# Rotated query and key parts: one copy in memory and twelve repeating strip reads per pair, in place of repeated copies and four reads

## The reference

```
x = x + attention(layernorm(x))
x = x + experts(layernorm(x))

# attention
q, k = rope(q), rope(k)
scores  = q @ k.T / sqrt(8), only where 0 <= i - j <= 63
weights = softmax(scores);  out = (weights @ v) @ Wout
```

## Time and profile before

| | us |
|---|---|
| median of 3 runs | 603.52 (600.43 to 605.98) |
| the profiled execution | 604.68 |
| its span, first to last instruction | 602.5 |

### The profile page before, as it was taken

One profiled execution on the slowest core, in us unless ns is written; L12 is line 12 of the kernel. 1 busy time (PEld: TensorE's weight loads), 2 busy tenths in 40 slices (PEclk: granted clock), 3 DMA queues, 4 the chain that ended last, 5 costly groups with the idle time before them and its releaser, 6 DMA issues.

```text
span 602.5 us, 20827 instructions
## 1 busy us (share of the span) xinstructions
PE 513.2 (85%) x7427; PEld 423.3 (70%) x7427; DVE 424.7 (70%) x1297; ACT 323.1 (54%) x832; POOL 343.0 (57%) x362
## 2 busy tenths in 40 slices
PE   3558997989988798887669889999989999999756
PEld 2336665766666566665545589999989999998544
DVE  5666799779999899966676366756666676664264
ACT  3336775767777677655546225455446555454200
POOL 8520113276666566655777507777777777777600
PEclk9659998989999999977899979999999999999977
DMA  7889998887877665520000134543534554541198
GB/s 254 234 234 249 250 248 235 225 268 212 240 231 208 210 209 151 137 66 25 21 12 10 36 99 140 150 123 108 164 119 140 171 155 149 170 118 49 24 394 292
DMA packets 79417, 98.33 MB, mean 163 GB/s; under 512 B 12097, under 2 KB 59999, under 8 KB 79216
## 3 DMA queue, kind: packets, MB, share of 16 engines
q1 hardware_dynamic: 65280, 82.92, 47.2%
q0 software_dynamic: 9216, 12.02, 6.4%
q10 hardware_dynamic: 4848, 2.40, 1.4%
HBM read 50.00 MB, written 54.30 MB: 173 GB/s over the span
## 4 chain that ended last, share of the span: by engine, by line
PE 38%; DVE 6%; DMA 5%; issue 4%; POOL 3%; ACT 2%; SPq 0%; POOLq 0%; DVEq 0%; ACTq 0%
PE banks L1115 18%; PE banks L1141 12%; DMA rload<-pair_results 3%; PE banks L1126 3%; POOL expert_slots L490 2%; DVE mx L1239 1%; PE banks L932 1%; DMA pair_results<-yout,yidx 1%; PE banks L1050 1%; POOL pair_results L618 1%; PE banks L1167 0%; DMA xg<-expert_slots 0%; SPq L440 0%; PE banks L874 0%; ACT yout L805 0%
## 5 line engine op out<-in xcount | busy, mean ns | idle before, releaser
L618 POOL DMA_INDIRECT pair_results<-yout,yidx x160 | 159.3, 996 | 67.0 <-issue 38.1
L490 POOL DMA_INDIRECT expert_slots<-xfe,sidx x128 | 127.8, 998 | 89.7 <-issue 38.9
L1115 PE MATMUL banks<-xgT_parts,wgu_parts 128*128 128x320 f32 x768 | 131.3, 320 | 1.9 <-DVE hact L1506 1.7
L1115 PEld LDWEIGHTS banks<-xgT_parts,wgu_parts 128*128 128x128 f32 x768 | 113.9, 190 | 4.6 <-DVE hact L1506 2.3
L1239 DVE TENSOR_REDUCE mx<-banks 128x8 f32<-128x1024 f32 x64 | 78.0, 1219 | 21.0 <-PE banks L882 21.0
L1506 DVE TENSOR_TENSOR hact<-hact,banks 128x320 f32<-128x320 f32 x128 | 56.6, 482 | 43.0 <-ACT hact L786 42.1
L805 ACT ACTIVATE yout<-banks,ypair 128x128 f32<-128x128 f32 x160 | 44.8, 372 | 76.2 <-PE banks L1141 73.8
L655 ACT ACTIVATE pt<-banks 128x512 f32<-128x512 f32 x128 | 69.3, 593 | 27.9 <-PE banks L913 26.6
L1141 PE MATMUL banks<-wdn,hact 128*128 128x128 f32 x640 | 76.6, 275 | 1.1 <-DVE hact L1506 1.1
L1141 PEld LDWEIGHTS banks<-wdn,hact 128*128 128x128 f32 x640 | 75.0, 192 | 1.3 <-issue 1.3
L786 ACT ACTIVATE hact<-banks 128x320 f32<-128x320 f32 x128 | 53.5, 452 | 33.1 <-PE banks L1115 31.4
(11 more groups left out here) (154 smaller groups left out, 945.5 us busy)
## 6 DMA issues: line engine op xcount, KB each, us to landing
expert_slots<-xg SPq DMA_DIRECT2D x32, 325.0 KB, 4.8
xg<-expert_slots SPq DMA_DIRECT2D x32, 325.0 KB
pair_results<-zero SPq DMA_DIRECT2D x32, 256.0 KB
rload<-pair_results SPq DMA_DIRECT2D x16, 512.0 KB, 8.9
kS<-rotated_keys SPq DMA_DIRECT2D x32, 240.0 KB
qS<-rotated_queries SPq DMA_DIRECT2D x32, 192.0 KB
wgu<-in_L_ffn_wg_dram SPq DMA_DIRECT2D x32, 128.0 KB
wgu<-in_L_ffn_wu_dram SPq DMA_DIRECT2D x32, 128.0 KB
```

Source lines behind the costliest of these rows:

```text
L490: g.indirect_dma_start(out=slots_d, out_offset=bass.IndirectOffsetOnAxis(ap=sidx[:, m % NB, j, k:k + 1], axis=0), in_=xfe[:, m % NB, j, k, ...
L618: g.indirect_dma_start(out=pairs_d, out_offset=bass.IndirectOffsetOnAxis(ap=yidx[:, c, j:j + 1], axis=0), in_=yout[:, c, j, :], in_offset= ...
L1115: last = mm(bank[2 + 2 * w + h][:, 0:CH], wgu_parts[:, e.b, wp, w, h * P:(h + 1) * P], xgT_parts[:, e.b, xp, ch * CH:(ch + 1) * CH], start ...
```

## The change

The tensors in memory hold three parts in place of six. `write_part` writes each part of queries and keys once. Each strip of 48 rows is read with three transfers, of 24, 16 and 8 rows, in place of one. For the queries (`Q_ROWS`), these repeat one part three times, the next twice, the last once: the source has an outermost dimension of stride zero. For the keys (`K_ROWS`), they read parts 0 to 2, then parts 0 and 1, then part 0. The six products are the same, in another order of rows. TensorE's wait counts twelve transfers per pair.

```diff
 NPART = 6
-Q_SLOTS = ((0, 1, 3), (3, 1, 2), (5, 1, 1))
-K_SLOTS = ((1, 2, 3), (0, 4, 2), (2, 1, 1))
+NSPLIT = 3
+Q_ROWS = ((0, 3, 0, False), (3, 2, 1, False), (5, 1, 2, False))
+K_ROWS = ((0, 3, 0, True), (3, 2, 0, True), (5, 1, 0, True))
 PEN_ROW = NPART * DH
+STRIP_LOADS = NS * (len(Q_ROWS) + len(K_ROWS))
...
-    q_d = nc.dram_tensor("rotated_queries", [NP, NPART, DH, NS, NG * PW], BF16, kind="Internal").ap()
-    k_d = nc.dram_tensor("rotated_keys", [NP, NPART, DH, NS, NG * (WIN + PW)], BF16, kind="Internal").ap()
+    q_d = nc.dram_tensor("rotated_queries", [NP, NSPLIT, DH, NS, NG * PW], BF16, kind="Internal").ap()
+    k_d = nc.dram_tensor("rotated_keys", [NP, NSPLIT, DH, NS, NG * (WIN + PW)], BF16, kind="Internal").ap()
...
             def write_part(m, a):
-                for w, (to, (first, step, count), lead) in enumerate(((q_d, Q_SLOTS[a], WIN), (k_d, K_SLOTS[a], 0))):
+                for w, (to, lead) in enumerate(((q_d, WIN), (k_d, 0))):
                     if w and a == 0:
                         sp.wait_ge(S.key_lead, m + 1)
-                    rows = to[m, first:first + step * (count - 1) + 1:step].rearrange("n d s (g t) -> (d s g) n t", g=NG)
-                    sp.dma_start(rows, parts[:, m % 2, a, w, lead:].unsqueeze(1)
-                                 .broadcast_to([P, count, WIN + PW - lead])).then_inc(S.qk_written, 16)
+                    sp.dma_start(to[m, a].rearrange("d s (g t) -> (d s g) t", g=NG), parts[:, m % 2, a, w, lead:])\
+                      .then_inc(S.qk_written, 16)
...
-                for strip, given in ((qS, q_d), (kS, k_d)):
+                for strip, given, rows in ((qS, q_d, Q_ROWS), (kS, k_d, K_ROWS)):
                     for s in range(NS):
-                        sp.dma_start(strip[STRIP * s:STRIP * s + PEN_ROW, m % NX].rearrange("p g t -> p (g t)"),
-                                     given[m, :, :, s].rearrange("r d t -> (r d) t")).then_inc(strips[m % NX], 16)
+                        for first, count, part, following in rows:
+                            at = STRIP * s + first * DH
+                            if following:
+                                source = given[m, part:part + count, :, s]
+                            else:
+                                source = given[m, part:part + 1, :, s].broadcast_to([count, DH, NG * PW])
+                            sp.dma_start(strip[at:at + count * DH, m % NX].rearrange("p g t -> p (g t)"), source)\
+                              .then_inc(strips[m % NX], 16)
...
-                        pe.wait_ge(strips[p % NX], 16 * 2 * NS * (p // NX + 1))
+                        pe.wait_ge(strips[p % NX], 16 * STRIP_LOADS * (p // NX + 1))
```

## The result

The changed kernel takes 627.74 us (median of 4 runs, 619.03 to 630.78), the kernel before 602.89 beside it (600.43 to 605.98): a ratio of 1.033, 95% interval 1.026 to 1.040. The ratio compares executions in the chip's faster state alone, for the changed kernel 625.40 and 619.03 of the four, with a mean of 622.2. By it the change costs 20 us. The forecast was 628, 23 us more than before; that 627.74 lies so close to it is luck in part. The profiled execution took 625.4 us, its span is 623.2 for 602.5, and these twenty-one microseconds can be followed from the prediction's own rows.

A forecast was written before the change was run, and what follows sets the result against it. Transfers were taken to bound the early stage, VectorE the later. Six early gaps +17, gap 6 to 7 +3, six later gaps +3, the end nothing: +23 on 604.7 gives 628 us, likeliest case's range 604 to 654.

The forecast's parts named there:

- What bounds the kernel: Attention pairs: transfers fill the DMA engines early (0.94 busy at 60 to 75 us), VectorE paces the later stage.
- The spread decides the sign: Strip reads: query reads run on three, two and eight engines, joined key reads on 12, 16 and 8; slower, total +23 us.
- The price of the narrow rows: Strip reads per pair: first engine's query rows 6.9 us, key rows 2.0; 9.0 us in place of 3.3.
- The early term: Six gaps between strip reads, pair 0 to 6: 17.4 us each, with weight loads 108.7 against 91.8, +17 us.
- The account: Gap between pairs' strip reads: one engine's reads, pieces and writes plus 1.9 us; 13.3 us before, 17.4 early after.
- The late gaps: Gap 6 to 7: 18.0 us against 14.9, +3; six gaps to pair 13: 16.7 against 16.2, +3.
- The end: After pair 13: 9.0 us of reads and 2 of latency fit 10.8 us of slack, so nothing; expert stage moves later unchanged.
- Issue: SP's queue: twelve strip reads for four at 0.42 us, last one 3.4 us later, hidden behind over 5 us of engine work.
- the rival without a difference: Reads spread evenly, but later issue costs 12 us over seven early steps against 11 saved: 605 us; chance 0.12.
- The faster rival: Reads spread over twelve or more engines, early gap 11.7 us, TensorE's strip stalls go: 597 us; chance 0.10.

The follow-up runs named there:

- the keys kept apart: Changed kernel with one unused row in memory behind each part of the keys, so part and dimension can't be joined into one count: 673.09 us, ratio 1.117.
- eight engines each: Changed kernel with the rows of each strip block reordered, head dimension (8) outermost, same writes, twelve reads and bytes: 629.43 us, ratio 1.044.
- half the writes: Kernel before, each part written once; four 48-row reads take the previous pair's rows instead of repeats, so output isn't the reference's: 596.74 us, ratio 0.989.
- the twelve even reads: Kernel before with its full writes, each 48-row strip read replaced by plain reads of 24, 16 and 8 rows: 613.67 us, ratio 1.018.
- the tiny reads: Kernel before with eight additional reads per pair, 16 rows of 64 B each to an unused tile, two ahead of each strip read: 631.49 us, ratio 1.042.

## Why the prediction was right, point by point

**What bounds the kernel.** Right: where the queue's pace changes, the first scores change with it, and the expert loop moves by 23.5 us, of which 2.8 come back by the end.

**The spread decides the sign.** Right, and shown from three sides: the packet counts fit to the last one (53536, 52800 with the keys kept apart, 53504 with eight engines each), a load on one engine that nobody waits for costs 1.034, and two badly divisible plain reads cost 1.035 with none of the change's other parts. That the narrow reads start from the same engine each time was assumed in the prediction. No record names an engine, but the numbers of packets under way show it: three while two reads are issued, then two.

**The price of the narrow rows.** The early term was +15.1 for +17, but that doesn't make the price right, since the terms overlap. With the keys narrow too, the five early gaps without weight loads average 20.2 us; less 8.4 for pieces, writes and latency that leaves 11.8 us for 313 kB, 38 us per MB, less than the undisturbed 40.5: part of the reading must go on during the other terms. By the packet records, the rows of that version take 13.6 us per pair (median, from the start of the first to the end of the last), 43 us per MB. In the changed kernel they take 9.1 to 11.2 us, waits for issues among them, with a median of 9.6 for the forecast 9.0. So the term was a little low. The account runs some 1.3 us short of the mean early gap where no engine is overloaded (14.6 for 13.3 before, 13.1 for 11.7 with half the writes) and is close where one is (16.9 for 17.4). The gap that it was held against, 13.2, is the shortest of the early ones, and it counts four fill pieces of 1.2 us per gap where SP issues five; whether that is what is short isn't shown. So it is luck in part that the total came out nearer than its terms.

**The late gaps.** +6.0 for +3: mis-sized. The sum let the strips land 2 us after 9.0 of reads and the last write 1.9 us after its issue. In the trace TensorE has the strips 11.8 to 13.4 us after the first issue: 1.5 us pass before the first row starts and some 0.6 after the last one. From the end of the last write's issue to the next strip read, 1.3 to 4.2 us pass, 3.2 on average for 2.5 before; 1.9 was the value of one quiet pair. That writes too stand behind narrow reads is the likely reason: behind pair 13's, from 245.1 to 247 us, the records show mostly one to three packets of the queue under way.

**The end.** The last three pairs gave 1.7 us back, which the sum didn't have (1.3 from the first read of pair 15 to its first scores, 0.4 in the two gaps before), and 2.2 of the 22.9 that are left at the last pair's first scores came back by the end.

**Issue.** Put at nothing because the first engine's load hides it: 3.4 us later for eight issues. It was 4.5 (5.8 for 1.3 in a quiet pair), since the query reads are issued at 0.59 us on average and not at 0.42. How much of the loss it would be alone was forecast as 1.7 us per early step in the rival without a difference; the twelve even reads show 1.9, with some uneven load among it. In the changed kernel the strips still land some 6 us after the last issue, so there the engine ends last. But the two are not shares of one sum: issues with little or no uneven load (1.018, and 1.042 with the tiny reads) and load alone (1.034, 1.035) each cost much, and with the load spread over eight engines the dearer issues took its place (1.044).

**The faster rival.** Its mechanism is real, and its size as worked out (596.7 for 597), where the reads stay as they are. What made it lose is the price of repeating on the reading side.

## What to carry to other kernels

Before splitting a transfer or repeating its source, look at the outermost count on both sides: three copies in front mean three engines, however many bytes there are, and a mean share over sixteen engines falls while the full one sets the pace. Where one queue paces a loop, each more issue and each more megabyte in it counts, even of transfers that nobody waits for. The bytes saved on the writes were worth 1% here; the same saving bought with a few unevenly spread and slowly issued reads cost 3%.

## What the runs showed of the hardware that was not expected

The issue of a read on SP takes about twice as long when its source keeps two counts of rows: 0.71 and 0.62 us for three and two parts, where plain reads of 24 and 16 rows took 0.29 to 0.35 (medians). The key reads went from 0.316 to 0.622 us when only a gap between their parts was added. It isn't the number of engines that makes it long: 29 plain rows on one engine were issued in 0.25 us.
